# A joint attention stage with its narrow weighing and output moved on TensorE, in a loop of four steps

## The reference

```python
# L2, wide: 16 heads of 64
h = layernorm(x) * gamma + beta
Q, K, V = h @ Wq, context @ Wk, context @ Wv          # 1024 columns each
attn = softmax(Q K^T per head) * 64 ** -0.5
x = x + (attn V) @ Wo
# L3, narrow: 16 heads of 8, no norm
q, k, v = x @ Wq.T, context @ Wk.T, context @ Wv.T    # 128 columns each
attn = softmax(q k^T * 8 ** -0.5)
x = x + (attn v) @ Wo.T + bo
```

## Time and profile before

| | |
|---|---|
| median of 3 runs | 1740.02 us (1736.38 to 1742.77) |
| the profiled execution | 1737.04 us, its span 1735.3 us |
| PE busy | 1632.6 us, 94% |
| DVE busy | 1315.0 us, 76% |
| ACT busy | 1244.4 us, 72% |
| POOL busy | 677.3 us, 39% |
| last stage | from about 1135 us to the end of the span |
| TensorE clock granted | 0.99 over the run |

### The profile page before, as it was taken

One profiled execution on the slowest core, in us unless ns is written; L12 is line 12 of the kernel. 1 busy time (PEld: TensorE's weight loads), 2 busy tenths in 40 slices (PEclk: granted clock), 3 DMA queues, 4 the chain that ended last, 5 costly groups with the idle time before them and its releaser, 6 DMA issues. The chain is left out here.

```text
span 1735.3 us, 48956 instructions
## 1 busy us (share of the span) xinstructions
PE 1632.6 (94%) x16520; PEld 1349.1 (78%) x16520; DVE 1315.0 (76%) x2408; ACT 1244.4 (72%) x3858; POOL 677.3 (39%) x946
## 2 busy tenths in 40 slices
PE   7999999999999999889899998978999999999997
PEld 6888888788888888779677777867787878787875
DVE  5777777777777777747588886656888888888885
ACT  4777777677777777623488886446888888888885
POOL 3444444454444444423222222633343434343431
PEclk9999999999999999999999999999999999999999
DMA  6777777777777667720000000013434343444441
GB/s 193 198 188 185 190 193 190 212 208 204 195 185 188 188 186 187 207 76 0 1 2 0 0 0 1 1 53 123 135 113 136 113 136 114 128 121 121 129 133 50
DMA packets 230717, 216.30 MB, mean 125 GB/s; under 512 B 19874, under 2 KB 228324, under 8 KB 230628
## 3 DMA queue, kind: packets, MB, share of 16 engines
q1 hardware_dynamic: 230628, 215.17, 44.7%
HBM read 112.34 MB, written 102.76 MB: 124 GB/s over the span
## 5 line engine op out<-in xcount | busy, mean ns | idle before, releaser
L658 ACT ACTIVATE L_probs<-L_scores,L_neg_max 128x128 f32<-128x128 f32 x512 | 182.7, 386 | 133.7 <-DVE L_neg_max L740 133.7
L854 POOL TENSOR_TENSOR L_probs<-L_probs,L_inv_sum 128x1024 f32<-128x1024 f32 x128 | 242.8, 1897 | 87.7 <-DVE L_inv_sum L760 87.7
L734 DVE TENSOR_REDUCE L_row_max<-L_scores 128x8 f32<-128x1024 f32 x128 | 156.2, 1220 | 42.4 <-PE L_scores L534 42.4
L1947 POOL TENSOR_TENSOR L2L_w_probs<-L2L_w_probs,L2L_w_inv_sum 128x1024 f32<-128x1024 f32 x64 | 121.4, 1896 | 156.1 <-DVE L2L_w_inv_sum L1774 156.1
L766 DVE STREAM_TRANSPOSE L_squares<-L_probs 128x1024 f32<-128x1024 f32 x128 | 156.7, 1224 | 0.3 <-POOL L_probs L854 0.3
L581 PE MATMUL L_ring<-L_probsT,L_v 128*64 128x128 f32 x2048 | 127.4, 276 | 10.1 <-issue 10.1
L581 PEld LDWEIGHTS L_ring<-L_probsT,L_v 128*64 128x64 f32 x2048 | 110.8, 137 | 30.5 <-issue 28.6
L534 PE MATMUL L_scores<-L_kT,L_qT 64*128 64x128 f32 x2048 | 131.8, 278 | 0.9 <-ACT L_kT L647 0.9
L534 PEld LDWEIGHTS L_scores<-L_kT,L_qT 64*128 64x128 f32 x2048 | 119.4, 188 | 12.5 <-ACT L_oT L647 8.2
L750 DVE TENSOR_REDUCE L_sums<-L_probs 128x8 f32<-128x1024 f32 x64 | 78.1, 1220 | 65.2 <-ACT L_probs L665 65.2
L1571 ACT ACTIVATE L2L_w_probs<-L2L_scores,L2L_w_neg_max 128x128 f32<-128x128 f32 x256 | 90.3, 370 | 45.6 <-DVE L2L_w_neg_max L1738 45.6
(11 more groups left out here) (220 smaller groups left out, 4610.8 us busy)
## 6 DMA issues: line engine op xcount, KB each, us to landing
L_relay<-L_squares SPq DMA_DIRECT2D x128, 512.0 KB, 3.4
L_probsT<-L_relay SPq DMA_DIRECT2D x512, 128.0 KB, 3.6
L2L_relay<-L2L_w_squares SPq DMA_DIRECT2D x64, 512.0 KB, 3.5
L2L_w_probsT<-L2L_relay SPq DMA_DIRECT2D x256, 128.0 KB, 2.9
out_x<-x SPq DMA_DIRECT2D x32, 64.0 KB, 2.8
L0a_wq<-in_L_xattn_Wq SPq DMA_DIRECT2D x2, 256.0 KB, 3.0
L0a_wk<-in_L_xattn_Wk SPq DMA_DIRECT2D x2, 256.0 KB, 3.9
L0a_wv<-in_L_xattn_Wv SPq DMA_DIRECT2D x1, 512.0 KB, 6.5
```

The costliest lines, as they stand in the source:

```text
L658: done = nc.scalar.activation(slot_probs(at, 0)[:, n, :], scores[:, 0, r, i, :], ACT.Exp, scale=layer_of(at).scale, bias=neg_max[:, n:n + ...
L734: nc.vector.tensor_reduce(row_max[:, s, :], slot(s), AX.X, ALU.max).then_inc(max_ready[s], 1)
L854: nc.gpsimd.tensor_tensor(to, to, inv_sum[:, :, s, :].unsqueeze(3) .to_broadcast([TOKENS, 2, GROUP, TOKENS]), ALU.mult).then_inc(divided, 1)
L1947: nc.gpsimd.tensor_tensor(to, to, w_inv_sum[:, :, s, :].unsqueeze(3) .to_broadcast([TOKENS, 2, GROUP, TOKENS]), ALU.mult).then_inc(w_divid ...
```

## The change

On TensorE the narrow weighing goes from ahead of n.hT to behind w.k1, w.hT goes from the end of the step to behind n.qk, and the narrow output goes from ahead of n.qk to between the two halves of the wide values. The table `order` follows. ScalarE copies n.hT ahead of the first narrow exponentials (before: behind) and does the second half of these behind n.qk (before: ahead). VectorE empties w.hT ahead of `w_add_up` and `n_finish` (before: behind both). The loop has a body of four steps and covers t = 4 to 27 in 6 turns; t = 4 and 27 stood outside it before. Step t's tail (t from 32) is as it was.

```diff
--- before.py
+++ after.py
@@ -1210,11 +1210,12 @@
 
     order = [("w.PV0", -1, "act"), ("w.PV1", -1, "act"), ("w.q0", 2, "act"), ("w.k0", 2, "act"),
              ("n.T0", -3, "act"), ("n.T1", -3, "act"), ("w.Wo", -1, "dve"), ("n.T2", -3, "act"), ("n.T3", -3, "act"),
-             ("n.iT", -3, "act"), ("n.PV", -3, "dve"), ("n.hT", -1, "act"), ("w.q1", 2, "act"), ("w.k1", 2, "act"),
-             ("n.Wo", -3, "dve"), ("n.qk", -1, "act"), ("w.v0", 1, "act"), ("w.v1", 1, "act"), ("n.v", -2, "act"),
-             ("w.hT", 3, "dve")]
+             ("n.iT", -3, "act"), ("n.hT", -1, "act"), ("w.q1", 2, "act"), ("w.k1", 2, "act"), ("n.PV", -3, "dve"),
+             ("n.qk", -1, "act"), ("w.hT", 3, "dve"), ("w.v0", 1, "act"), ("n.Wo", -3, "dve"), ("w.v1", 1, "act"),
+             ("n.v", -2, "act")]
     first, last = -4, BATCHES + 2
-    steady_first, steady_last = 5, BATCHES - 5
+    TURN = 4
+    steady_first, steady_last = 4, BATCHES - 5
 
     tail_order = [("w.PV0", -1, "act"), ("w.PV1", -1, "act"), ("w.Wo", -1, "dve"), ("n.T0", -3, "act"),
                   ("n.T1", -3, "act"), ("n.hT", -1, "act"), ("n.T2", -3, "act"), ("n.T3", -3, "act"),
@@ -1322,7 +1323,14 @@
             engine.wait_ge(emptied[ring.engine[name]], ring.count(name, at))
 
         def steps(engine, step):
-            pipeline(engine, step, first, last, steady_first, steady_last)
+            for t in range(first, steady_first):
+                step(At(t))
+            with engine.Fori(0, (steady_last + 1 - steady_first) // TURN) as turn:
+                i = turn * TURN
+                for k in range(TURN):
+                    step(At(steady_first + k, i))
+            for t in range(steady_last + 1, last + 1):
+                step(At(t))
 
         def w_slot(at, s):
             return w_probs[:, at.n % 2, s, :, :]
@@ -1533,22 +1541,24 @@
                     n_transpose_probs(t.plus(-3), 2)
                     n_transpose_probs(t.plus(-3), 3)
                     n_transpose_inverses(t.plus(-3))
-                    n_weigh(t.plus(-3))
                 if here(t, -1):
                     n_transpose_h(t.plus(-1))
                 if here(t, 2):
                     w_queries_keys(t.plus(2), 1)
                 if here(t, -3):
-                    n_project_out(t.plus(-3))
+                    n_weigh(t.plus(-3))
                 if here(t, -1):
                     n_queries_keys(t.plus(-1))
+                if here(t, 3):
+                    w_transpose_h(t.plus(3))
                 if here(t, 1):
                     w_values(t.plus(1), 0)
+                if here(t, -3):
+                    n_project_out(t.plus(-3))
+                if here(t, 1):
                     w_values(t.plus(1), 1)
                 if here(t, -2):
                     n_values(t.plus(-2))
-                if here(t, 3):
-                    w_transpose_h(t.plus(3))
 
             steps(pe, step)
 
@@ -1677,17 +1687,16 @@
                     n_turned_probs(t.plus(-3), 2)
                     n_turned_probs(t.plus(-3), 3)
                     n_turned_inverses(t.plus(-3))
+                if here(t, -1):
+                    n_turned_h(t.plus(-1))
                 if here(t, -2):
                     n_exponentiate_0(t.plus(-2), 0)
-                if here(t, -1):
-                    n_turned_h(t.plus(-1))
                 if here(t, 2):
                     w_projections(t.plus(2), 1)
-                if here(t, -2):
-                    n_exponentiate_0(t.plus(-2), 1)
                 if here(t, -1):
                     n_projections(t.plus(-1))
                 if here(t, -2):
+                    n_exponentiate_0(t.plus(-2), 1)
                     n_exponentiate_1(t.plus(-2))
                 if here(t, 1):
                     w_values(t.plus(1), 0)
@@ -1877,12 +1886,12 @@
                     n_weighted(t.plus(-3))
                 if here(t, -2):
                     n_subtract_maxima(t.plus(-2))
+                if here(t, 3):
+                    w_turned_h(t.plus(3))
                 if here(t, 1):
                     w_add_up(t.plus(1))
                 if here(t, -3):
                     n_finish(t.plus(-3))
-                if here(t, 3):
-                    w_turned_h(t.plus(3))
                 if here(t, -2):
                     n_invert(t.plus(-2), 0)
 
@@ -1908,7 +1917,8 @@
                 if at.n >= 1:
                     pool.wait_ge(n_x_bias_ready, at.times(1, 0))
                     await_filled(pool, "n.hT", at.plus(-1))
-                nc.gpsimd.tensor_copy(n_rows_h[:, :], x[:, at.index, :]).then_inc(n_rows_h_ready, 1)
+                rows = x[:, at.index, :] if at.i is None else x[:, 1:, :][:, at.times(1, -1), :]
+                nc.gpsimd.tensor_copy(n_rows_h[:, :], rows).then_inc(n_rows_h_ready, 1)
 
             def w_add_bias(at):
                 if at.n >= 2:
```

## The result

| | changed kernel | kernel before, same runs |
|---|---|---|
| median of 5 runs | 1730.1 us (1727.46 to 1735.21) | 1741.49 us (1736.38 to 1742.77) |
| ratio, with its 95% interval | 0.9944 (0.9931 to 0.9957) | |
| profiled execution, its span | 1727.86 us, 1726.1 us | 1737.04 us, 1735.3 us |
| PE busy | 1638.1 us, 95% | 1632.6 us, 94% |
| DVE, ACT, POOL busy | 1310.8, 1240.9, 677.3 us | 1315.0, 1244.4, 677.3 us |

The kernel is faster. 1740.02 times the ratio is 1730.3 us, inside the range, with a gain of 9.7 us instead of 15.0. Lines of PE are 8 higher than before: the weighing is L1464 and n.hT L1483. POOL's copy for n.hT is L1921.

The account below looks back on a forecast made before the run. TensorE, busy 94 to 96%, was taken to set the step's length. Exchange 12.0, loop 2.3 and last steps 0.7 sum to 15.0 us, so 1740.02 becomes 1725.0 us, range 1716 to 1736.

Parts of the forecast that it names:

- The weighing's wait, taken away: PE's narrow weighing in each last-stage step no longer waits for ScalarE's copies: 0.78 us saved per step.
- n.hT's wait, new: PE's n.hT now waits for POOL's copy: 0.16 us in a written-out step, 0.36 in a looped one.
- The exchange of the two: Weighing's wait gone less n.hT's new wait: 0.62 us per written-out step, 0.42 per looped, 12.0 us over steps 3 to 29.
- The loop: Six turns of four steps instead of 11 of two: five times 0.45 us, 2.3 us saved, bounds nothing to 2.3.
- The gap of 0.33 at the jump: PE stays idle for about 0.33 us between turns of the loop, six times.
- First and last steps: Steps up to t = 2: nothing, between 1 us lost and gained. Last steps from t = 30: 0.7 us gained.
- Covers: Time to spare for moved work: 0.35 us before w.v0, 0.5 before the wide scores, 1 before n.Wo.
- Rival 1: POOL's copy for n.hT comes in time, so n.hT does not wait: 9.1 us more gained, 1716 us; chance 0.06.
- Rival 2: A new wait, at n.hT or where thin covers are used up: 1734 to 1740 us; chance 0.15.
- Rival 3: PE's larger loop body is fetched again at each jump: 34 us for five jumps, 1759 us; chance 0.06.

Follow-up runs that it names:

- Experiment 5: Also copyfirst2: turn2 with POOL's n_copy_rows ahead of w_add_bias instead of behind it; ratio to the kernel before 0.9861, median 1716.39 us.
- Experiments 5 to 7: After 5, 6: new order, last stage written out without a loop, ratio 0.9902; 7 (second unrolled kernel): also POOL's n_copy_rows ahead of w_add_bias, 0.9875.
- experiments 1 to 4: 1: turn2, 0.9927. 2: changed kernel, ScalarE alone looping two steps, 0.9932. 3: act4, 0.996. 4: kernel before with a four-step loop, 1.0005.
- act4: Changed kernel with ScalarE alone on a four-step loop body, the other engines on two; ratio to the kernel before 0.996.
- turn2: Also experiment 1: changed kernel with a loop body of two steps on all engines; ratio to the kernel before 0.9927, median 1726.12 us.
- whT_last2: turn2 with w.hT back at the end of the step, on TensorE and VectorE; ratio to the kernel before 1.018.
- weigh_only2: turn2 with n.Wo directly behind the weighing and w.hT, its VectorE part too, at the step's end; ratio to the kernel before 1.0055.
- experiment 8: The run weigh_only2: turn2 with n.Wo directly behind the weighing and w.hT at the step's end; ratio to the kernel before 1.0055.

## Why the prediction was right in its range and short in its sum

- **The weighing's wait, taken away.** Right. No row of L1464 waits in the loop. In the written-out step the weighing starts at +12.92, where +12.8 was forecast; in the looped one at +13.19 (1386.78 - 1373.59), where the same sum with POOL's later copy gives +13.0.
- **n.hT's wait, new.** Right in place and time: +11.06 forecast for a looped step and +11.10 found, +10.85 and +10.88 for a written-out one. Experiment 5 shows it from the other side: the copy one place earlier takes the wait away and 0.27 to 0.31 us off each looped step (17.13 and 17.17 to 16.86).
- **The exchange of the two: mis-sized.** The net was put at 0.62 us in a written-out step and 0.42 in a looped one. It is 17.34 - 16.85 = 0.49, and 17.42 - 17.12 = 0.30 (the old looped steps alternate between 17.42 and 17.70, the longer with the jump). Over 24 and 3 steps this is 3.3 us less than the 12.0. What failed is the assumption that the operations take as long in the new order as in the old, so that each idle stretch taken from PE shortens the step by its full length. PE's busy time in a step rose from 16.66 to 16.77 and 16.82 with the same instructions. With the weighing behind it, w.k1 takes 0.99 (1386.78 - 1385.79), where with the output behind it it took 0.89; this 0.10 stands in every kernel of the new order, whether n.hT waits or not, and is most of the missing 0.13. The rest is n.hT, 0.03 to 0.04 later than forecast. And n.hT's wait does not count in full: w.q1 takes 1.00 when PE has not waited just before, so that the first 0.2 us of it cost nothing. Experiments 5 to 7 agree on 16.85 to 16.86, with n.hT early (5 and the second unrolled kernel) or 0.24 us later (the first).
- **The loop: wrong in sign.** Forecast: 2.3 us saved. Measured in the profiles: the ten old jumps cost 0.28 us each, 2.8 in all, and the five new first steps cost 5.6, so 2.8 lost. (The term was too large in itself as well: five saved jumps at 0.28 are 1.4 us; the rest of the 0.45 was the longer looped step, 17.42 against 17.34, which a larger body does not save.) The prediction asked of PE's queue whether the larger body is fetched again, and answered rightly that it is not. It did not ask it of the other engines. ScalarE's body grew from 148 to 292 records, and it is ScalarE's that is fetched (experiments 1 to 4). My bounds, nothing to 2.3 saved, had no loss in them. In medians the fetch costs 5.5 us between act4 and turn2 on one chip (1731.62 and 1726.12), 4.0 between the changed kernel and turn2.
- **The gap of 0.33 at the jump** was forecast six times and came not once. I took it for a property of the jump, but turn2's two steps differ by 0.04 us. whT_last2 and weigh_only2, both with w.hT at the end of the step, have it again, 0.33 us 12 times and 0.27 us 11 times. So the gap shows when the step ends with that single transposition. Why it does is not shown.
- **First and last steps.** The first were put at nothing, between a loss and a gain of 1 us, and gained 3.5 in this pair. Of these, 2.0 lie where the order is the same in both kernels, 1.6 of them at a lower granted clock before. The steps -1 to 2 gained 1.5, by t = 1 (22.82 to 20.13 us). The four kernels with w.hT last have 22.67 to 22.82 us there and the eight with w.hT early 17.75 to 20.26. The steps -1 to 2 together take 56.99 us in whT_last2 and 55.16 in turn2, which differ in that move alone, so it is worth 1 to 2 us there, at or above the bound of 1 us that was given for it. The last were put at +0.7 and came at -0.4: n.Wo's wait in the tail fell from 1.7 to 0.5 us, but others took it up.
- **Covers.** All held. No wait stands at the wide values or the scores, thin as they were (0.35 and 0.5 us). VectorE's wait for w.hT, 16.9 us before, is gone. The product for n.Wo starts at +14.53 in a written-out step where about +13.9 was forecast, which takes 0.6 of its 1 us of cover.
- **Rival 1** (POOL in time) did not come by itself, and copyfirst2 made it come: 1716.39 us against the 1716 written for it. That the two agree is luck: by the rival's sum a looped step would take 16.64 us and it takes 16.86, while the loop of two and the first steps make up for that. **Rival 2** stands partly: no cover broke, but the wait at n.hT is 0.75 instead of 0.30 in the first step of a turn, when ScalarE is late. **Rival 3** did not occur on PE at four steps. Its mechanism is real: on ScalarE at four steps with about 1 us a turn, and on PE at six with 5 to 6 us. Of the Trainium skill's two rules (Runtime: NRT & Kernel Launch, Instruction fetch mechanics), the one of a window of two pages is not borne out for PE: a body of 1607 records loops over five jumps with a single q8 packet, ahead of the first of them. Its figure of 2048 instructions for TensorE agrees with both runs: four steps are inside, six, an estimate of 2400, outside. For the other engines it gives 512, and there that figure alone does not decide: ScalarE's body of 292 records is fetched again. The 292 include the register operations, semaphores and the branch that left a record; whether the body holds more than its records stays open.

The terms add up so, in the profiled pair: 15.0 forecast, less 3.3 for the exchange, less 5.1 for the loop (2.3 hoped for, 2.8 lost), less 1.1 at the end, and 3.5 more at the start make 9.0, beside the 9.2 measured. So the time came as near the forecast as it did partly by luck: a gain that was not forecast, 2.0 us of it no gain of the change, made up for part of what was missing.

What each part is worth in the end, from the ratios: weighing behind w.k1 alone +0.55% (experiment 8), with output and w.hT moved -0.73% (experiment 1), the loop of four +0.17% on top (the intervals of the two ratios overlap; act4 against turn2 has +0.33%), and against turn2 one exchange on POOL -0.66% (0.9861 to 0.9927).

## What to carry to other kernels

A loop body is fetched by each engine for itself: count the instructions of each, and read q8 and q14 inside the loop before and after the body grows. When a wait of the bounding engine is taken away, look at what its operations take behind their new neighbours and when it hasn't waited, since short waits can cost nothing; and look at what its new neighbour waits for, since one operation moved on POOL brought nearly as much here (0.66%) as the whole reordering (0.73%). Parts of a reordering that each look optional may hold each other up by their buffers, so undo them one by one.

## What the runs showed of the hardware that was not expected

- With a body of 292 records, ScalarE's instructions are fetched again in each turn, some five packets of 8 KB (q14, 0.24 MB in 29), and it stands for about 1 us, 1.41 at the longest, in the middle of a step. With 148 records it does not. Five packets seem more than the body: PE's 235 records to a packet of 16 KB make some 70 bytes a record, by which 292 records would be an estimate of 2.5 packets of 8 KB. How much of the body comes again, and what comes beside it, stays open. PE, with packets of 16 KB (q8, 0.59 MB in 36), does not at 1607 records and does at six steps. Where between the two each of them lies wasn't tried.
- PE makes up for a wait of 0.24 us at n.hT by the start of w.k1, the next fill but one (experiments 6 and 7).
- ScalarE's stop during a fetch is told by the trace as a wait for PE, whose matmuls had been done. Only the queue showed what it was.
